# A quantised convolution and two DISCO convolutions on one core: the work before the first convolution is shared out anew among VectorE, ScalarE and GpSimd

## The reference, cut to what matters

```python
def _gn(v, G=16, eps=1e-05):           # group norm, 16 groups of 2 channels, per image
    g = v.reshape(B_, G, C_ // G, H_, W_)
    m = mean(g); s = var(g)            # over channels of the group, rows, columns
    return ((g - m) / sqrt(s + eps)).reshape(v.shape)

def _L0_conv_ref(x, weight, bias):     # 3x3 convolution on int8 values
    qx, sx = quantize(x)               # sx = max|x| over the WHOLE batch, q = round(x*127/sx)
    qw, sw = quantize(weight)
    return conv(qx, qw) * (sx * sw / (127 * 127)) + bias

def _disco_conv(x, w):                 # w: 32 x 32 x 36, PSI: 36 x 3 x 3, fixed
    return conv(x, einsum('oik,khw->oihw', w, PSI))

x = x + _L0_conv_ref(_gn(x), L0_conv_weight, L0_conv_bias)
h = instnorm_lrelu(_disco_conv(_gn(x), weight1))
x = x + instnorm_lrelu(_disco_conv(h, weight2))
```

## Time and profile before

| what | us |
|---|---|
| median of 3 runs | 413.42 (412.99 to 413.45) |
| the profiled execution, its own time | 413.55 |
| its span in the trace | 411.4 |
| PE busy in the span | 311.0 (76%) |
| DVE busy | 313.6 (76%) |
| ACT busy | 233.1 (57%) |
| POOL busy | 86.5 (21%) |

### The profile page before, as it was taken

One profiled execution on the slowest core, in us unless ns is written; L12 is line 12 of the kernel. 1 busy time (PEld: TensorE's weight loads), 2 busy tenths in 40 slices (PEclk: granted clock), 3 DMA queues, 4 the chain that ended last, 5 costly groups with the idle time before them and its releaser, 6 DMA issues.

```text
span 411.4 us, 11773 instructions
## 1 busy us (share of the span) xinstructions
PE 311.0 (76%) x5344; PEld 127.7 (31%) x5344; DVE 313.6 (76%) x483; ACT 233.1 (57%) x225; POOL 86.5 (21%) x154
## 2 busy tenths in 40 slices
PE   0001010375999999999999999999999999997970
PEld 0000000335343334333333433343343334333520
DVE  5977999786468879778976977997698879557144
ACT  1589993523244766286468527654844766285434
POOL 0011377103220303120330304033011300100000
PEclk9999999996999999999999999999999999999995
DMA  8999200000000023005000500220050013005005
GB/s 297 413 429 422 118 0 2 0 2 2 2 3 2 2 77 131 3 2 205 3 2 3 206 3 2 117 92 2 4 206 3 2 79 131 2 3 206 2 2 204
DMA packets 4177, 34.78 MB, mean 85 GB/s; under 512 B 608, under 2 KB 768, under 8 KB 1280
## 3 DMA queue, kind: packets, MB, share of 16 engines
q1 hardware_dynamic: 4128, 34.04, 20.2%
HBM read 17.26 MB, written 16.78 MB: 83 GB/s over the span
## 4 chain that ended last, share of the span: by engine, by line
PE 52%; DVE 32%; ACT 7%; issue 5%; POOL 2%; DMA 1%; DVEq 0%; SPq 0%; POOLq 0%
PE ring L766 36%; DVE bn_c L636 10%; PE ring L818 8%; DVE xs L653 7%; DVE qpad L613 4%; DVE amax L568 3%; PE ring L725 3%; PE ring L772 3%; ACT hpad L293 2%; ACT apad L280 2%; ACT hpad L288 2%; PE gathered_in L718 1%; DVE own_stat_c L643 1%; DVE bn_x L626 1%; DVE xs L620 1%
## 5 line engine op out<-in xcount | busy, mean ns | idle before, releaser
L636 DVE BATCH_NORM_STATS2 bn_c<-ring 128x6 f32<-128x512 f32 x128 | 82.7, 688 | 60.4 <-PE ring L772 60.4
L317 ACT COPY apad<-ring 128x1024 f32<-128x1024 f32 x32 | 32.2, 1006 | 63.1 <-DVE bn_c L636 63.1
L766 PE MATMUL ring<-hpad,own 64*32 64x512 f32 x512 | 67.1, 592 | 0.0
L772 PE MATMUL ring<-apad,own 64*32 64x512 f32 x512 | 67.0, 592 | 0.0
L766 PE MATMUL ring<-apad,own 64*32 64x512 f32 x512 | 67.0, 592 | 0.0
L772 PE MATMUL ring<-hpad,own 64*32 64x512 f32 x512 | 66.8, 592 | 0.0
L766 PE MATMUL ring<-hpad,vert 64*32 64x512 f32 x512 | 66.7, 588 | 0.0
L772 PE MATMUL ring<-apad,side 64*32 64x512 f32 x512 | 66.5, 587 | 0.0
L766 PE MATMUL ring<-apad,vert 64*32 64x512 f32 x512 | 66.4, 587 | 0.0
L772 PE MATMUL ring<-hpad,side 64*32 64x512 f32 x512 | 66.3, 588 | 0.0
L718 PE MATMUL gathered_gn<-spread_x,const 128*128 128x24 f32 x32 | 8.4, 346 | 66.8 <-DVE spread_x L554 60.1
(11 more groups left out here) (97 smaller groups left out, 468.6 us busy)
## 6 DMA issues: line engine op xcount, KB each, us to landing
xs<-x_dram SPq DMA_DIRECT2D x8, 2048.0 KB, 9.8
out_dram<-xs SPq DMA_DIRECT2D x14, 1024.0 KB, 3.9
out_dram<-xs SPq DMA_DIRECT2D x4, 512.0 KB, 2.9
xs<-w_dram SPq DMA_DIRECT2D x1, 288.0 KB, 3.5
const<-const_dram SPq DMA_DIRECT2D x1, 146.0 KB, 3.0
xs<-w_dram SPq DMA_DIRECT2D x1, 36.0 KB, 3.3
bias<-bias_dram SPq DMA_DIRECT2D x1, 0.5 KB, 3.0
```

Of the source, the lines that this page charges most:

```text
L317: nc.scalar.copy(unit_of(tile, u), grid(slot(FIRST[v] + u))).then_inc(taken[v], 1)
L636: ins = nc.vector.bn_stats(bn[s][:, u * UBANKS + h, :], ring[:, (FIRST[v] + u) % SLOTS, h, :])
L766: nc.tensor.matmul(bank_out(u, v, hp, C * (2 * px + py), C), wv[q0:q0 + 64, v - 1, px, py, :], window(tile, u * UBANKS + hp, dy, 0, q0, 64 ...
L772: ins = nc.tensor.matmul(bank_out(u, v, hx, C * (2 * px + py), C), ws[q0:q0 + 64, v - 1, px, py, :], window(tile, u * UBANKS + hx, 0, dx, ...
```

## The change

The DISCO taps leave DVE. POOL makes them now: 15 products into a new scratch `w_prod`, then 10 additions and one copy into `kern`, which is a tile of its own and no longer lies in `scaled`. `w12` is loaded after image 0. Images 0, 1 and 4 have their sums from DVE; images 2, 3, 5, 6 and 7 have them from ACT, which now also writes the members with the mask itself (`spread_act`). POOL normalises all images, but for the second half of image 7, which ACT does. Scratch tiles are three: `apad[0]`, `apad[1]` and `hpad`. ACT's unused output goes to the inside of `qpad`. ACT assembles `kern0` after its sums, and both fp32 kernels after the quantised pieces of image 0; PE waits for these only before period 0. The gathers run in the order 0, 1, 2, 4, 3, 5, 6, 7. The maximum of image 7 is taken in halves.

```diff
+PRODUCTS = 15
+X_SUMS = [2, 3, 5, 6, 7]
+X_ORDER = [0, 1, 2, 4, 3, 5, 6, 7]
+GN_ORDER = [0, 1, 2, 3, 4, 5, 6, 7]
...
-        kern = scaled[0][0:C, 0:2 * TAPS * C]...
+        kern = sb("kern", [P, 2 * TAPS * C], F32)[0:C]...
...
+        gn_tiles = [apad[0], apad[1], hpad]
+        gn_cut = COLS // 2
 SP
-            sp.dma_start(w12...).then_inc(small_in, 16)
             sp.dma_start(w0, ...); bias; const
-            for b in range(B):
+            load(0)
+            sp.dma_start(w12...).then_inc(w12_in, 16)
+            for b in range(1, B):
 ...
-                    sp.wait_ge(kernels_ready, 1)
+                    sp.wait_ge(kern_done, 1)
+                    sp.wait_ge(kern0_done, 1)
 ACT
+            junk = rows_of(qpad, 0, BLK)
+            def x_sums(b, n):
+                act.wait_ge(x_in[b], 16)
+                if n > 0:
+                    act.wait_ge(x_squared, n)
+                nc.scalar.activation(junk, grid(xs_cols(b, 0, COLS)), ACT.Identity, scale=1.0 / (BLK * COLS),
+                                     accum_out=own_x[:, b, 1:2]).then_inc(x_meaned, 1)
+                act.wait_ge(x_meaned, n + 1)
+                nc.scalar.activation(junk, grid(xs_cols(b, 0, COLS)), ACT.Square, bias=own_x[:, b, 1:2],
+                                     scale=-1.0 / BLK, accum_out=own_x[:, b, 2:3]).then_inc(x_squared, 1)
+                act.wait_ge(x_squared, n + 1)
+                if n >= 2:
+                    act.wait_ge(gathered["x"], X_ORDER.index(X_SUMS[n - 2]) + 1)
+                nc.scalar.activation(spread_act[:, n % 2, :, 1], mask_mean[:], ACT.Identity, scale=own_x[:, b, 1:2])
+                nc.scalar.activation(spread_act[:, n % 2, :, 2], mask["x"][:, :, 2], ACT.Identity,
+                                     scale=own_x[:, b, 2:3]).then_inc(spread_sums, 1)
...
+            for n, b in enumerate(X_SUMS):
+                x_sums(b, n)
+            act.wait_ge(kern0_done, 1)
+            assemble(kern0, own0, side0, vert0, corn0).then_inc(weights0_ready, 1)
+            act.wait_ge(norm_ready["x"], B)
+            act.wait_ge(max_done, GN_ORDER.index(B - 1) - 2)
+            nc.scalar.activation(gn_tile(B - 1)[:, gn_cut:], xs_cols(B - 1, gn_cut, COLS - gn_cut), ACT.Identity,
+                                 bias=..., scale=...).then_inc(gn_half, 1)
 ...
             for n in range(4):
                 affine0(n)
+            act.wait_ge(kern_done, 1)
+            assemble(kern[:, 0], ...)
+            assemble(kern[:, 1], ...).then_inc(weights12_ready, 1)
 POOL
+            pool.wait_ge(w12_in, 16)
+            ... 15 x last = nc.gpsimd.tensor_scalar(w_prod[:, n], w12[:, :, k, :], float(psi[k, ty, tx]), 1.0, ALU.mult, ALU.mult)
+            last.then_inc(products_done, 1)
+            pool.wait_ge(products_done, 1)
+            pool.wait_ge(w0_step, 2)
+            ... 6 x tensor_tensor add of pairs, 1 x add and 1 x copy into taps; a wait; 3 x tensor_tensor add into taps
+            last.then_inc(kern_done, 1)
+            def gn_x(b):
+                cols = gn_cut if b == B - 1 else COLS
+                pool.wait_ge(norm_ready["x"], X_ORDER.index(b) + 1)
+                if GN_ORDER.index(b) >= 3:
+                    pool.wait_ge(max_done, GN_ORDER.index(b) - 2)
+                nc.gpsimd.tensor_scalar(gn_tile(b)[:, 0:cols], xs_cols(b, 0, cols), gn_scale[:, b:b + 1],
+                                        gn_shift[:, b:b + 1], ALU.mult, ALU.add).then_inc(gn_done[b], 1)
+            for b in (0, 1, 2):
+                x_params(b)
+                gn_x(b)
+            x_params(4)
+            x_params(3)
+            gn_x(3)
+            gn_x(4)
+            for b in (5, 6, 7):
+                x_params(b)
+                gn_x(b)
 DVE
-            ... the 15 linked instructions that made the taps, x_spread_sums
+            x_stats(0); x_spread(0, 0); x_group(0)
+            x_stats(1); x_spread(1, 1); x_group(1)
+            x_max(0, 0)
+            x_group(2)
+            x_stats(4); x_spread(4, 2); x_group(4)
+            x_group(3)
+            x_max(1, 1); x_max(2, 2)
+            x_group(5)
+            x_max(3, 3); x_max(4, 4)
+            x_group(6)
+            x_max(5, 5)
+            x_group(7)
+            x_max(6, 6)
+            x_max(7, 7, 0, gn_cut)
+            x_max(7, 8, gn_cut, COLS)
 PE
-            pe.wait_ge(weights_ready, 1)
+            pe.wait_ge(weights0_ready, 1)
             pe.wait_ge(amax_step, 1)
             keep_clock(KEEP_Q, 0)
-            for t in range(-1, B + 1):
+            period(-1)
+            pe.wait_ge(weights12_ready, 1)
+            for t in range(B + 1):
                 period(t)
```

More of the change, by code:

```diff
@@ L159, in conv_block_kernel @@
         small_in = sem("small_in")
+        w12_in = sem("w12_in")
         x_in = [sem(f"x_in{b}") for b in range(B)]
-        w_step = sem("w_step")
+        w0_step = sem("w0_step")
         wmax_done = sem("wmax_done")
[L163 to L169, removed]
+        products_done = sem("products_done")
+        tap_step = sem("tap_step")
+        kern_done = sem("kern_done")
+        kern0_done = sem("kern0_done")
+        weights0_ready = sem("weights0_ready")
+        weights12_ready = sem("weights12_ready")
+        mask_scaled = sem("mask_scaled")
+        x_meaned = sem("x_meaned")
+        x_squared = sem("x_squared")
+        x_aggregated = sem("x_aggregated")
+        gn_done = [sem(f"gn_done{b}") for b in range(B)]
+        gn_half = sem("gn_half")
+        max_set = sem("max_set")
+        max_done = sem("max_done")
         amax_step = sem("amax_step")
@@ L215, in slot, with gn_tile @@
             return ring[:, n % SLOTS, :, :].rearrange("p b c -> p (b c)")
-        POOL_GN = [*range(2, B, 2), B - 3]
-        def x_moments(par):
-            return moments_x2 if par else moments["x"]
+        gn_tiles = [apad[0], apad[1], hpad]
+        def gn_tile(b):
+            return flat(gn_tiles[b % 3])
+        gn_cut = COLS // 2
         FIRST = {1: 0, 0: UNITS, 2: 2 * UNITS}
@@ L236, in _ @@
             sp.dma_start(const[:], const_d[:, :]).then_inc(small_in, 16)
[L237 removed]
+            load(0)
+            sp.dma_start(w12.rearrange("p v k o -> p (v k o)"), w12_d[:, :]).then_inc(w12_in, 16)
+            for b in range(1, B):
                 if b >= 2:
@@ L270, in assemble @@
                 return last
[L272 to L281, removed]
@@ L484, in _ @@
                 nc.vector.memset(tile[:], 0.0)
-            for s in STAGES:
+            for s in STAGES[1:]:
                 nc.vector.memset(own_stat[s][:, 0:1], 1.0)
             nc.vector.memset(minus_half[:], -0.5)
[L488 to L502, removed]
@@ new lines, in _ @@
+            x_stats(0)
+            x_spread(0, 0)
+            x_group(0)
+            x_stats(1)
+            x_spread(1, 1)
+            x_group(1)
+            x_max(0, 0)
+            x_group(2)
+            x_stats(4)
+            x_spread(4, 2)
+            x_group(4)
+            x_group(3)
+            x_max(1, 1)
+            x_max(2, 2)
+            x_group(5)
+            x_max(3, 3)
+            x_max(4, 4)
+            x_group(6)
+            x_max(5, 5)
+            x_group(7)
+            x_max(6, 6)
@@ L823, in conv0_pair @@
                 ins.then_inc(conv_done[0], 1)
-            for b in range(B):
-                gather("x", b)
+            counts = [0, 0]
+            for i, b in enumerate(X_ORDER):
+                if i > 0:
+                    pe.wait_ge(moments_ready["x"], i)
+                n = counts[b in X_SUMS]
+                counts[b in X_SUMS] += 1
+                if b in X_SUMS:
+                    pe.wait_ge(spread_sums, n + 1)
+                    rhs = spread_act[:, n % 2]
+                else:
+                    pe.wait_ge(spread_ready["x"], n + 1)
+                    rhs = spread["x"][:]
+                nc.tensor.matmul(gather_ps["x"], gather_w["x"], rhs.rearrange("p j e -> p (j e)"),
+                                 start=True, stop=True).then_inc(gathered["x"], 1)
             def period(t):
```

183 lines of the change are left out of this document (90 added, 93 removed).

## The result

The changed kernel took 409.27 us in the median of 5 runs (408.46 to 411.13), against 413.42 for the kernel before (412.99 to 413.62). The ratio is 0.9908, with a 95% interval of 0.9891 to 0.9924. That is a gain of about 4 us where 7.8 were forecast. The profiled execution took 408.46 us for a span of 406.7.

The account below looks back on a forecast made before the run. Everything PE does hangs on `amax1`, the end of DVE's maxima, with ACT's sums and POOL's taps close by. `amax1` from 78.73 to 70.9, less 7.8 us: 413.42 - 7.8 = 405.6; range 403.8 to 409.6.

Parts of the forecast that it names:

- first-use cost: POOL's first TENSOR_SCALAR started 3.82 us after its moments; taken as paid once, charged to the first tap product.
- rival A: POOL's 11.52 us idle runs from the first all-reduce; first product at 17.7, `amax1` 74.3, time 409.0; chance 0.20.
- T: Time at which the DISCO taps end on POOL: forecast 22.0 us, or 18.2 without the first-use cost.
- The landings: Image loads with `w12` behind image 0: image 0 at about 10.0, `w12` 10.7, images 2 and 4 staying at 21.1 and 30.9.
- The way from T to `amax1`: Image 0 normalised, its maximum, `x_stats(4)` at T + 9.7, then 38.6 us of DVE without a gap; above 22, T + 49.1.
- image 6 on POOL: POOL's tightest normalisation: group made at 56.0, normalised at 61.2, wanted by DVE at 61.6; a little late in the 70.9.
- The taps' own price: Tap instructions on POOL: 16 with one input at 0.22 us, 10 with two at 0.35; 7.0, with waits 7.5.
- An image of sums on ACT: ACT's two passes over an image, 7.53 us, plus two small member activations, 0.35: 7.9 us an image.
- The first point from which the taps count: End of the taps on POOL: below 21 they cost nothing, above 22 each us moves the end by one.
- The fp32 assemblies: 24 copies on ACT behind the quantised pieces, 4.8 us, hidden in 14.20 us of ACT idle; uncovered, up to 4.8.
- Rival B: POOL's late start plus every tap instruction at the power's 0.55 us: taps end 32.0, `amax1` 81.1, 415.8 us; chance 0.05.
- Rival C: Behind `amax1`, the granted clock's rise does not move with the work; some matmuls run slow, 1.7 us: 407.3; chance 0.08.

Follow-up runs that it names:

- the probe: Changed kernel with one more 128x1 TENSOR_SCALAR on POOL directly behind the second all-reduce, where no image is being loaded: 408.75 us, a single run.

## Why the prediction was wrong

**The step that failed is the start of the first product on POOL.** The prediction took 3.8 us of "issue" as a first-use cost, charged it once, behind the landing of `w12`, and got a start at 14.5. It was 17.43. The reading that fits stood in rival A, with a chance of 0.20: the 11.52 us of idle in the earlier trace rows run from the all-reduce. A gave T = 25.2 and `amax1` = 74.3; measured were 25.14 and 74.42. That agreement is partly luck. A kept the 11.52 and let the all-reduce end at 6.2. The all-reduce ended at 7.79, though its input was there at 4.49 (6.05 us lay between a TENSOR_SCALAR and it when one was put ahead), and the gap was 9.6: two errors of 1.6 and 1.9 us that cancelled. What gave A its small chance was "an engine that is idle should have loaded what it needs". The runs show otherwise: the time begins behind the all-reduce, whatever ran before it, and it does run on while POOL waits for `w12` or for moments. The 3.82 us were merely the part that stuck out behind the moments at 17.44.

Of the Trainium skill, the GPSIMD Engine Reference (Instruction dispatch) says that the first call to a freshly loaded kernel pays about 6 us, with no instruction in the profile. The trace agrees that no instruction shows it, and in the size ahead of the second all-reduce: 5.7 to 6.1 us in the changed kernels. Behind an all-reduce it was longer, 7.4 us in the probe and 9.6 to 12.0 while images load. What the prediction missed in that sentence is "freshly loaded": the program goes back and forth between the all-reduce and the tensor instructions, and in these runs the time was paid at each such change. That code is fetched in that time is the page's account; the runs show only when the time is paid and how long it is.

**The landings were the second error.** With `w12` behind image 0, image 0 landed at 10.97 and not 10.0, `w12` at 12.35 and not 10.7, and images 2 and 4 at 21.93 and 31.83, 0.8 and 0.9 later than before, where the prediction had "stay". In the six profiles with `w12` behind image 0, image 2 landed at 21.9 to 22.6, in the seven with it ahead at 20.3 to 21.7. In the changed kernel this cost nothing beside the taps. Without the taps' delay it is the whole of the 1.9 us between 72.09 and 70.23, since ACT's sums begin at 22.26 and at 20.41.

**The way from T to `amax1`** was forecast as T + 49.1 and measured as T + 49.28, but the 49.1 is not the sum of the prediction's own parts. Those are T + 9.7 and 38.6, so 48.3, and 48.9 with image 6 on POOL "a little late". Measured are T + 9.76 and 39.52 from there (34.90 to 74.42). What the 38.6 lacked are two waits for POOL: 0.73 us for image 6 at 65.42, and 0.37 for the TENSOR_TENSOR at 40.12, a wait that the prediction did not have at all; what is left ran 0.2 us faster than forecast. It named the opposite as its risk, that POOL's instructions slow down beside DVE's `bn_stats`; the taps took 7.7 us beside them, and 7.8 where they ran mostly ahead of them (4.43 to 12.24).

**What was right.** The taps' own price, 7.5 against 7.7 us, though by luck in its parts: one input was put at 0.22 us and took 0.29, two inputs were put at 0.35 and took 0.29. An image of sums on ACT: 7.9 against 7.97 (five starts from 22.00 to 53.87). Writing to rows of `qpad` costs nothing: the passes take 3.60 to 3.62 and 3.71 us, as before. The first point from which the taps count, 22, is confirmed only in that 20.5 is below it and 24.8 above. Image 6 on POOL was called the tightest, and it was. The fp32 assemblies hid as said: ACT then still idled 9.52 us before its next work, at 95.67. Rival B can be dropped, for a two-input addition costs 0.29 us. Rival C did not come either: the granted clock was back at 97.21, ahead of the first DISCO matmul at 98.73.

**Behind `amax1`.** The time from there to the end of the span was 332.7 before and 332.3 in the profile of the changed kernel. In the other kernels it was 332.1 to 333.7, with 333.7 for the changed kernel itself, run again. So the profiled execution was a short one, and the median (409.3, then 410.1) lies above it. The 1.4 us between the two profiles of the changed kernel lie behind 100 us, nearly all in PE's busy time (columns as in the earlier trace rows; the first line is the first profile, the second the repetition):

```profile
100.00:406.00 306.00, 287.44 (x5082) 110.26 (x5066) 230.76 (x346) 170.65 (x157) 56.08 (x101) 0.98 0.14 57
100.20:407.60 307.40, 288.89 (x5082) 111.34 (x5066) 230.82 (x346) 170.77 (x157) 56.18 (x102) 0.97 0.14 57
```

The same 5082 matmuls took 1.45 us longer at a mean granted clock of 0.97 and not 0.98. That the clock makes the difference is likely from these rows, but no run was made for it. A new wait was missed: POOL's last normalisation now ends at 68.82, and the second all-reduce starts 5.96 us later, 0.36 us behind `amax1` instead of 0.13 (0.60 without the first all-reduce).

**In us.** 7.8 were forecast for `amax1` and 4.3 came. Of the missing 3.5, 3.1 are T (25.14 against 22.0); the rest, 0.4, is the way from there to `amax1`, 49.3 us against the 48.9 between 22.0 and 70.9, about the 0.37 by which POOL held the TENSOR_TENSOR.

## What to carry to other kernels

An idle time on GpSimd that the profile calls "issue" should be measured from both of its ends: from what the instruction waited for, and from the instruction before it on the engine. Count the changes between partition all-reduce and ordinary tensor instructions in GpSimd's list. In this kernel each cost 6 to 12 us of that engine, which is free while it idles anyway and is paid in full once work is moved behind it. Before moving work to the engine that looks most idle, ask when it becomes able to start, not how long it is busy, and what it then holds up: here a pass on POOL held a TENSOR_TENSOR of DVE that met it, until the pass ended.

## What the runs showed of the hardware

- Between a partition all-reduce and the next TENSOR_SCALAR on GpSimd lay 9.6 to 12.0 us while 16.8 MB of images were loading (nine profiles of eight kernels), and 7.4 with no load on the way. A MEMSET in between ran at once (7.34, behind an all-reduce begun at 7.05).
- In the other direction 5.7 to 6.1 us lay between the last TENSOR_SCALAR and the second all-reduce in the kernels where the all-reduce started later behind `amax1` than the 0.13 us of the kernel before (changed kernel: end at 68.82, start at 74.78, 0.36 behind `amax1`). At the start of the program a TENSOR_SCALAR ran at 1.13 without any such wait, while the first all-reduce never ran before 6.98.
- A DVE TENSOR_TENSOR of 128x24 elements that met a POOL TENSOR_SCALAR over 128x4096 ended 0.02 to 0.04 us behind it in nine profiles: it took 2.84 us in one, 2.51 in another, 0.53 to 0.68 in seven, against 0.18 to 0.26 where it met none. No experiment was made on it.
- With 288 KB loaded behind the first 2 MB image, image 2 landed at 21.9 to 22.6 us, with them loaded ahead of it at 20.3 to 21.7, though the bytes were the same. Why was not tried.
